# Seven fast relations instead of five in an RGCN kernel: sums seeded in PSUM, sums of x made in the first unit

## The reference, cut to what matters

```python
def _rgcn(x, edge_index, edge_type, weight, root, bias):   # x: layernorm of the input, 625 x 1024
    src, dst = (edge_index[0], edge_index[1])
    msgs = x[src]
    out = x @ root + bias
    for r in range(8):
        mask = (edge_type == r).astype(x.dtype)
        sums = segment_sum(msgs * mask[:, None], dst)
        cnt = segment_sum(mask, dst)
        out = out + (sums / maximum(cnt, 1.0)[:, None]) @ weight[r]
    return out
```

## Time and profile before

| | us |
|---|---|
| median of 3 runs (1108.13 to 1110.11) | 1108.44 |
| the profiled execution | 1113.76 |
| its span | 1112.0 |
| PE busy | 1066.2 (96%) |
| DVE busy | 793.0 (71%) |
| POOL busy | 417.4 (38%) |
| ACT busy | 413.9 (37%) |

### The profile page before, as it was taken

How to read it: one execution, slowest core, us unless ns; L and a number is a source line. 1 busy time by engine, 2 the same in 40 slices (tenths; PEclk the granted TensorE clock), 3 DMA queues, 4 the chain that set the end, 5 groups by cost and what they waited for, 6 DMA issues and landing times.

```text
span 1112.0 us, 14475 instructions
## 1 busy us (share of the span) xinstructions
PE 1066.2 (96%) x5385; PEld 891.4 (80%) x5385; DVE 793.0 (71%) x1591; ACT 413.9 (37%) x647; POOL 417.4 (38%) x272
## 2 busy tenths in 40 slices
PE   6998999999999999999999998999979999999995
PEld 5776887777787777889999998887756878888774
DVE  7567888889989897317667776495479648876647
ACT  3331333434434343122332323361443415256652
POOL 6023488788788888212442330000010000410016
PEclk9999999999999999999999999999989999989998
DMA  9999978788977776799999742523242201588757
GB/s 322 400 331 383 327 181 145 193 218 208 223 193 147 196 140 161 169 244 219 271 261 252 170 126 99 208 83 126 60 80 89 76 2 59 223 281 277 235 180 258
DMA packets 94475, 217.34 MB, mean 195 GB/s; under 512 B 29978, under 2 KB 46173, under 8 KB 85947
## 3 DMA queue, kind: packets, MB, share of 16 engines
q1 hardware_dynamic: 39488, 137.19, 36.5%
q0 software_dynamic: 37504, 48.18, 21.8%
q10 hardware_dynamic: 17406, 30.97, 10.1%
HBM read 149.59 MB, written 66.71 MB: 195 GB/s over the span
## 4 chain that ended last, share of the span: by engine, by line
PE 78%; DVE 10%; DMA 6%; ACT 3%; issue 1%; ACTq 1%; POOLq 0%; SPq 0%; DVEq 0%
PE ps L583 65%; PE ps L891 3%; PE ps L928 3%; DVE rl L414 3%; DVE EQ L1578 3%; DMA stage<-in_w_e 2%; PE ps L855 2%; DMA stage<-in_w_rel 2%; DMA KR<-key_scratch 2%; PE ps L573 1%; ACT rh L405 1%; DVE V L1498 1%; ACT He L1106 1%; PE ps L939 1%; PE ps L906 1%
## 5 line engine op out<-in xcount | busy, mean ns | idle before, releaser
L2219 POOL DMA_INDIRECT adj_scratch<-cnt,idx x164 | 288.9, 1762 | 133.8 <-issue 43.6
L414 DVE TENSOR_TENSOR rl<-stage,rh 128x512 fp32r<-128x512 f32 (+1 forms) x264 | 213.4, 837 | 152.3 <-ACT rh L405 148.7
L405 ACT CAST rh<-stage 128x512 fp32r<-128x512 f32 (+1 forms) x264 | 180.4, 716 | 364.9 <-PE ps L583 242.8
L583 PE MATMUL ps<-rh,xTh 128*125 128x512 f32 x600 | 239.0, 398 | 5.7 <-ACT He L1106 4.6
L583 PE MATMUL ps<-rl,xTh 128*125 128x512 f32 x600 | 237.5, 396 | 0.0
L583 PE MATMUL ps<-rh,xTl 128*125 128x512 f32 x600 | 237.4, 396 | 0.0
L583 PE MATMUL ps<-rh,Ar 125*125 125x342 f32 x600 | 190.8, 323 | 5.4 <-issue 4.0
L583 PE MATMUL ps<-rl,Ar 125*125 125x342 f32 x600 | 190.3, 322 | 0.0
L583 PEld LDWEIGHTS ps<-rh,xTh 128*125 128x125 f32 x600 | 112.0, 187 | 35.9 <-ACT He L1106 7.2
L583 PEld LDWEIGHTS ps<-rh,xTl 128*125 128x125 f32 x600 | 112.1, 187 | 28.4
L583 PEld LDWEIGHTS ps<-rl,xTh 128*125 128x125 f32 x600 | 112.0, 187 | 27.4
(11 more groups left out here) (295 smaller groups left out, 1615.1 us busy)
## 6 DMA issues: line engine op xcount, KB each, us to landing
stage<-in_w_rel SPq DMA_DIRECT2D x22, 1024.0 KB, 6.4
stage<-h_scratch SPq DMA_DIRECT2D x24, 855.0 KB, 7.3
stage<-in_w_e SPq DMA_DIRECT2D x16, 1024.0 KB, 6.6
adj_scratch<-Z POOLq DMA_DIRECT2D x16, 767.0 KB, 20.1
adj_scratch<-Z SPq DMA_DIRECT2D x16, 767.0 KB, 16.1
h_scratch<-He ACTq DMA_DIRECT2D x40, 257.0 KB, 9.1
h_scratch<-He ACTq DMA_DIRECT2D x40, 256.0 KB, 4.7
KR<-key_scratch ACTq DMA_DIRECT2D x37, 256.0 KB, 6.5
```

The costliest lines, as they stand in the source:

```text
L405: e.copy(h, s).then_inc(*a_hi.up(*[("hi", t) for t in step(i)]))
L414: e.tensor_tensor(l, s, h.bitcast(F32), ALU.subtract).then_inc(*v_lo.up(*[("lo", t) for t in step(i)]))
L583: ins = e.matmul(ps[0:P, b, 0:width], a, m, start=first and n == 0, stop=last and n == len(parts) - 1, skip_group_check=again)
L2219: e.indirect_dma_start(accd[to], bass.IndirectOffsetOnAxis(ap=idx[:, n:n + 1], axis=0), cnt[:, n:n + 1], None, compute_op=ALU.add).then_in ...
```

## The change

Units 2 and 3 become fast too, so seven of the eight relations are. The sums of x that they need move from units 2 and 3 into unit 1: the first set between the copies of its first half, the second set behind its tiles. In all fast units three of the adds on DVE go into PSUM: ACT writes W into the bank of X, minus X into the bank of Z and minus E1 into that of E2 (`seed`), and PE adds its products to that. V2 and V3 then are plain copies on ACT in place of adds on DVE; the last three results of a unit are copied by ACT in place of subtracted by DVE; the copy V5 is gone. Of the 41 key windows 21 stood in units 1 to 3 and four in each of the five fast units; now two stand in unit 1 and 39 in the fast units (six a unit, five in units 6 to 8). SP loads b22 and b21 of unit 2 before b11 and b12, and starts the zero stores of copy 1 with the loads of unit 3.

```diff
-WINDOWS = {(0, 1): (0, 2, 4, 6), (1, 0): (0, 1, 2, 4, 5, 6), (1, 1): (0, 2, 4), (2, 0): (2, 4, 6), (2, 1): (0, 2, 4, 6),
-           (8, 0): (), (8, 1): ()}
+WINDOWS = {(0, 1): (4, 7), (8, 0): (), (8, 1): ()}
...
-FAST = (4, 5, 6, 7, 8)
+FAST = (2, 3, 4, 5, 6, 7, 8)
+SEEDED = (("X", 0), ("X", 1), ("Z", 0), ("Z", 1), ("E", 2))
...
-KEYS_IN_FAST = {u: (3, 10, 17, 24) for u in FAST}
-S_IN = ((1, 1), (2, 0))
+KEYS_IN_FAST = {u: (2, 7, 12, 16, 21, 25) if u < 6 else (2, 8, 13, 18, 24) for u in FAST}
...
-            for g in range(2, first("h", 0, 0, 0)):
+            ahead = [fast_loads[FAST[0]][kind] for kind in ("b22", "b21")]
+            for g in (2, 3, *ahead, *(g for g in range(4, first("h", 0, 0, 0)) if g not in ahead)):
...
-                if 6 <= g < 10:
+                if 8 <= g < 12:
...
+                    if start and seeded:
+                        before_seed[u, role] = old
+                        on.wait_ge(*at("seed", u, role))
...
+            def seed(u, role, source, sign, ready):
+                to, b = (ps[0:P, banks.of["fast", u, *name], :] for name in (role, source))
+                on.wait_ge(*at(*ready))
+                for ev in before_seed[u, role]:
+                    on.wait_ge(*at(*ev))
+                e.activation(to, b, ACT.Copy, scale=sign).then_inc(*a_out.up(("seed", u, role)))
...
                     if i - F0[u] == 13:
                         for p in range(2):
-                            on.wait_ge(*at("fast", u, "b11", ("W", p)))
+                            seed(u, ("X", p), ("W", p), 1.0, ("fast", u, "b11", ("W", p)))
+                    if i - F0[u] == 17:
+                        for p in range(2):
+                            on.wait_ge(*at("fast", u, "t2", ("X", p)))
...
+                            e.copy(V2[0:P, p, :], ps[0:P, banks.of["fast", u, "X", p], :]).then_inc(*a_out.up(("v2", u, p)))
+                            seed(u, ("Z", p), ("X", p), -1.0, ("fast", u, "t2", ("X", p)))
+                        seed(u, ("E", 2), ("E", 1), -1.0, ("fast", u, "b11", ("E", 1)))
...
+                    if n == 0 and hf == 0:
+                        for c in range(C - 1):
+                            s_high(c, 0)
+                            h_copy(unit, c, hf, banks.of["unit", unit, hf, c], "unit", unit, hf, c)
+                            h_store(unit, c, hf)
+                        highs(unit_tile(unit, 1, 7) + 1)
+                        h_copy(unit, C - 1, hf, banks.of["unit", unit, hf, C - 1], "unit", unit, hf, C - 1)
+                        h_store(unit, C - 1, hf)
+                        for s in range(4):
+                            s_high(s, 1)
+                        continue
...
-                    if i - F0[u] == 17:
-                        for p in range(2):
-                            on.wait_ge(*at("fast", u, "t2", ("X", p)))
-                            on.wait_ge(*at("v1", u, p))
-                            e.tensor_tensor(V2[0:P, p, :], ps[0:P, banks.of["fast", u, "X", p], :], V2[0:P, p, :], ALU.add).then_inc(*v_out.up(("v2", u, p)))
...
-                for c in (0, 2, 4):
-                    on.wait_ge(*at("he", FAST[-1], c, 1))
+                for c in (1, 3):
+                    on.wait_ge(*at("he", FAST[-1], c, 0))
```

More of the change, by code:

```diff
@@ L511, in sync @@
                             *d_kr_first[kg].up(("kr", kg)))
[L512 removed]
+                if 8 <= g < 12:
                     on.wait_ge(*at("Z"))
[L514 removed]
+                    for a in range(4 * (g - 8), 4 * (g - 7)):
                         e.dma_start(adj_zeros[1][a], Z[:]).then_inc(*d_zero[1].up(("adj zero", 1)))
@@ L645, in part @@
                     b, old = held[role]
+                    seeded = role in SEEDED
                     on.wait_ge(*at("lo", i))
-                    for ev in (*ready, *(old if start else ())):
+                    if start and seeded:
+                        before_seed[u, role] = old
+                        on.wait_ge(*at("seed", u, role))
+                    for ev in (*ready, *(old if start and not seeded else ())):
                         on.wait_ge(*at(*ev))
-                    return three(b, i, stat, start, stop, kind in ("t4", "b21", "b22"))
+                    return three(b, i, stat, start and not seeded, stop, seeded or kind in ("t4", "b21"))
                 def ends(ins, kind, j, role, last_role):
@@ L660, in fast_unit @@
                 for p in range(2):
-                    held["X", p] = banks.take(("fast", u, "X", p), ("v2", u, p), where=of.get(("X", p)))
+                    held["X", p] = banks.take(("fast", u, "X", p), ("v2", u, p), ("seed", u, ("Z", p)), where=of.get(("X", p)))
                 for p in range(2):
@@ L1133, in fast_between @@
                             h_store(u, c, 0)
-                    if i - F0[u] == 39:
+                    if i - F0[u] == (36 if u == FAST[-1] else 37):
+                        for p in range(2):
+                            h_copy(u, 2 * p, 1, banks.of["fast", u, "Z", p], "fast", u, "b22", ("Z", p))
+                        h_copy(u, 4, 1, banks.of["fast", u, "E", 2], "fast", u, "b22", ("E", 2))
                         for c in (0, 2, 4):
@@ L1646, in vector @@
                                 g += 1
-                            if (n, hf) in S_IN and k % 2:
-                                s_made(k // 2, S_IN.index((n, hf)))
-                        if (n, hf) == S_IN[1]:
-                            s_low(3, 1)
                     elif n == 0:
-                        key_window(g)
-                        g += 1
+                        for s in range(4):
+                            s_made(s, 0)
+                        lows(unit_tile(unit, 1, 7) + 1)
+                        for s in range(4):
+                            s_made(s, 1)
+                        s_low(3, 1)
                     if unit == 0:
```

42 lines of the change are left out of this document (13 added, 29 removed).

## The result

The changed kernel takes 1117.59 us (median of 11 runs, 1114.6 to 1123.28); the kernel before took 1110.38 beside it (11 runs, 1108.13 to 1115.91). The ratio is 1.0072, 95% interval 1.0047 to 1.0098: slower by some 7 us, where 7 us faster was forecast. The profiled execution took 1117.59 us as well.

What follows compares the result with a forecast made beforehand. PE was taken to bound the kernel. The later of P (494.1) and A (491), less 499.7 and 1.4, gave -7.0 us; from the median 1108.4 that made 1101.4 us, range 1093 to 1112.

Steps and rivals of the forecast that it cites:

- Its law: The spread starts at the later of P and A; before, these were 499.7 and 488.15 us.
- P: Time when PE has done the root, ahead of the spread; forecast 494.1 us, bounds 489 and 503.
- 0 to 6 us; I take 1.5, since 135 is the middle: Unit 3: DVE stands at b21, landing between 132 and 140 behind zero stores; 1.5 us added to P.
- The first seeds: Unit 2's t2 waits for its seeded bank until about 92 instead of 83.0: 9 us, 1.5 more at lower clock.
- Fewer matmuls and old waits: 48 fewer matmuls in two units take 11.1 us off P; old waits gone from units 1 to 3, 6.5 off.
- wait of 4.07: PE's old wait at 110.05, 4.07 us plus 1.5 for slow matmuls, counted among the old waits that go.
- Seeds and DVE: Seeds cost nothing up to 1.1 us each; DVE, 93% busy in units 3 to 5, costs nothing in steady state.
- Both rivals built on them: DVE as bound in units 3 to 8, or seed copies over 1.1 us; together 0.12.
- A: Time when the first `Ar`, the adjacency, is there for the spread; forecast 491 us, bounds 471 and 508.
- adjacency decides: Rival at the spread's start: A is late, decides from 494 and makes the kernel slower from 501; chance 0.23.
- What stands behind the start of the spread is unchanged: After the spread's start the forecast let only a 1.4 us wait go and kept the rest as before.
- The wait of 1.44 us: After the spread's first fifty matmuls PE waited for DVE's low part beside POOL's add; assumed gone, 1.4 us off.

Runs made afterwards that it cites:

- e3: Changed kernel with ACT's loads of key rows one window later; median 1115.5 us, ratio 1.0049 to the kernel before.
- e18: Changed kernel with half of copy 1's zero stores ahead, two behind each unit 3 load, plus e3's edit; median 1117.2 us, ratio 1.0021 to before.
- e4: Changed kernel with the edits of e1 and e3 together; median 1129.1 us, ratio 1.0190 to the kernel before.
- e6: Changed kernel with the edits of e2 and e3 together; median 1107.4 us, ratio 0.9942 to the kernel before.
- e1: Changed kernel with all 16 zero stores of copy 1 moved behind unit 3's b21 load; median 1136.2 us, ratio 1.0249 to the kernel before.
- e13: e6 with POOL's seven sums of the adjacency cut to 8 columns; median 1107.5 us, ratio 0.9957 to the kernel before.
- e2: Changed kernel with all 16 zero stores of copy 1 right behind unit 2's b12 load; median 1110.2 us, ratio 1.0010 to the kernel before.
- e5: e2 with each of ACT's seeds written twice; one run, spread started at 495.0 us, 2.9 later than e2's.
- e10: Changed kernel with ACT's cast of the second adjacency behind the high part of the spread's second group; median 1119.8 us, ratio 1.0068 to before.
- e9: e6 with ACT's cast of the second adjacency behind the high part of the spread's second group; median 1111.6 us, ratio 0.9968 to before.
- e7: e2 with key window 0 on DVE moved into unit 1's first half; median 1105.1 us, ratio 0.9946 to the kernel before.
- e17: Changed kernel with half of copy 1's zero stores ahead and two behind each load of unit 3; median 1127.1 us, ratio 1.0121 to before.
- e12: Kernel before with ACT's cast of the second adjacency behind the high part of the spread's second group; ratio 0.9975 to before.
- e15: Kernel before with POOL's sums of the adjacency cut to 8 columns; median 1109.1 us, ratio 0.9995 to before.
- e14: Changed kernel with POOL's sums of the adjacency cut to 8 columns; median 1116.7 us, ratio 1.0060 to the kernel before.
- e8: Changed kernel with copy 1's zero stores ahead, unit 2 plain, eight key windows in unit 1's second half and unit 2; ratio 1.0147 to before.

## Why the prediction was wrong, step by step

**Its law held up to the spread.** The start was max(P, A) in every kernel of the table, within 0.2 us. For the changed kernel P decided, as forecast, at 501.8 in place of 494.1.

**The term that failed is unit 3: "0 to 6 us; I take 1.5, since 135 is the middle".** It measured 10.73, and 2.4 for the lower clock behind it. The mechanism was named (b21 last but for four stores, DVE standing at it); both ends of it were off. b21 landed at 142.0, 7 us behind the middle that I took and 2 behind the range of 132 to 140. And the chain behind it was not written down: the half sum of t4, a low part, a key window, a low part, the second half sum of t3, three high parts and then the seed, 150.97 - 142.01 = 9.0 us, the same in e3 and e18. By the prediction's own times PE would have come to this t2 at 83.0 + 9 + 1.5 + 50.0 = 143.5, so b21 was due at 134.5; PE came at 140.2, so it was due at 131.2. The 10.7 us are 0.5 for a landing at 135, 7.0 for the later landing and 3.3 for the earlier PE. DVE's stop of 4.72 us at b22 adds nothing of its own, since without it DVE would have stood at b21 that much longer. With this term at its measured size, 1.5 replaced by 10.7 and 2.4, P was 505.7, 4 us too much; of these the first seeds give 2.4 and PE's arrival at them, at 81.7 in place of 83.0, 1.3.

**The first seeds.** Predicted 9 (7 to 14) and 1.5; measured 6.78 and 1.3. b12 came at 67.5 in place of 70 and key window 1 ended at 87.2 in place of 89.5. Mechanism and place were right (e3, e4 and e6 each took 3 to 4 us off, and e18 4.5, by moving the load of key rows alone).

**Fewer matmuls and old waits** went as forecast: 5337 matmuls, and no wait of 4.07. From PE's arrival at unit 2's t2, 88.48 - 6.78 = 81.7, there are 1716 matmuls to the spread: 1716 x 0.2315 = 397.3; with the two waits, 17.5, and 3.7 at the lower clock the start comes out at 500.2, 1.6 below the trace.

**Seeds and DVE.** No wait in units 4 to 8; the pair of seeds ahead of t2 takes 1.06 us in units 2 and 3, and doubling all seeds cost 2.9 us in seven units. Both rivals built on them fell.

**A.** Predicted 491 (group 5 at 160), measured 492.1 (158.2). That it came so near is in part luck: group 5 was 1.8 us earlier than predicted, and the shorter wait behind the last adds (7.5 in place of 12.3) gave 4.8 us where 7 had been taken. The rival "adjacency decides" did not occur in this kernel, but its rule did as soon as the stores were moved back: 510.2 in e1. From group 5 on the adds took 297 to 307 us in the kernels with seven fast units, 304 before; the fuller DVE did not slow them. What is stretched is large elementwise work on both sides: beside POOL's sum of 6.34 us a low part of DVE takes 7.5 to 8.6 us in place of 1.94, and without the sum it takes 1.94 (e13). The rule of the Trainium skill, "SBUF — State Buffer" (SBUF: two separate sides), an exclusive lock between a DVE operation with two SBUF inputs and a POOL operation that reads SBUF, agrees with these rows; on POOL's adds, where the prediction feared it, no effect is seen (1.68 us in the median, 1.70 before).

**"What stands behind the start of the spread is unchanged"** held for the changed kernel only up to "layers" (848.1, 346.3 us behind the start, before 346.4). The wait of 1.44 us is gone as assumed, but the stretch is only 0.1 us shorter, so that this term of the sum brought nothing. Where P and A lie close, or A decides, the stretch itself is longer: 346 to 348 us with A at least 6 us ahead (changed, e2, e3, e5, e10), 354 at 2.6 (e9), and 358 to 360 where PE waits for `Ar` (e1, e4, e6, e7, e17, e18).

**The sum against the median.** The trace gives 3.8 us in the span: 2.3 at the start and 1.5 at the end. The medians differ by 7.2, since the profiled run of before was 3.4 above its own median. The traces near the medians (e12 and e15 for before's order, the changed kernel and e14) have 262.2 and 262.8 us from "layers" to the end against 267.7 and 268.8, and there the difference is in the landing of the experts' weights. (e14's profiled run lay 2.9 above its median.) In all twenty traces this part took from 261.4 to 270.2 us, with the same work in it. So the 14 us between forecast and median are some 8 of a later start (11.6 for unit 3, less 3.7 for the first seeds), 1.3 of the wait that brought nothing, and some 5 behind "layers". Why that part should be longer in the median of the changed kernel, by some 5 of its 7 us, stays open: sums left out, another order on ACT and other places of the stores did not show it. So does why e18's median lies 7 us further above before's than e6's, with nearly the same trace.

## What to carry to other kernels

When bulk stores are moved between loads, cost each load by all bytes ahead of it in its queue, compare its landing with the consumer's arrival, and then follow the chain from the landing to the last engine: the wait is the landing plus that chain, less the time at which that engine arrives, and an engine that arrives earlier than planned waits longer. A transfer that nobody waits for has a due time as well (here the zeroed second copy of the adjacency), so look for a gap in the queue early in the program before spreading it over the loads. And where two chains end within 10 us of each other, a gain on one is paid only up to the other, and here part of it was lost again at a second meeting a little further on.

## What the runs showed that I had not expected

A copy from PSUM to PSUM on ACT of 125x512 takes 583 ns in the mean of 35 in the changed kernel, and one from PSUM to SBUF (`He`) 588 in the mean of 52. The Trainium skill, "ScalarE: Activation LUTs" (Step-by-step: what each stage is for), has PSUM as the faster target; in this trace the difference is 5 ns. A low part of 1.94 us stretched to 8.63 (e17) beside a POOL sum of 6.34. And sixteen zero stores of 767 KB, put ahead of two weight loads, held PE for 32 us (e8), while in e2, where none of the next loads stands behind them, they cost it 1.7 us.
